# Loading per-edge data for four groups at once, and unrolling the loops of five engines to eight groups, in the second layer of a graph network

## The reference, cut to what matters

```
x[src]                                  # 32 features of the source, gathered
h = relu(w * w1 + b1)                   # 64 hidden values of the edge
R = [h, 1] @ w2m                        # 384 values of the edge
msg = products of R with x[src] and with x[src] turned by the frame (3 x 3)
out[dst] += msg                         # segment sum, here a scan along the sorted edges
```

## Time and profile before

| | us |
|---|---|
| median of three runs | 22618.37 |
| lowest and highest | 22526.03, 22643.42 |
| profiled execution, its span | 22701.8 |

### The profile page before, as it was taken

One profiled execution on the slowest core, in us unless ns is written; L12 is line 12 of the kernel. 1 busy time (PEld: TensorE's weight loads), 2 busy tenths in 40 slices (PEclk: granted clock), 3 DMA queues, 4 the chain that ended last, 5 costly groups with the idle time before them and its releaser, 6 DMA issues. The chain is left out here.

```text
span 22701.8 us, 347931 instructions
## 1 busy us (share of the span) xinstructions
PE 13867.1 (61%) x118841; PEld 8367.2 (37%) x118841; DVE 11327.4 (50%) x19891; ACT 2921.4 (13%) x4729; POOL 11857.2 (52%) x10101
## 2 busy tenths in 40 slices
PE   0465555555554767767676334444444449999999
PEld 0244433333333444444444222222222225555554
DVE  2665544444444777777777422222222234555554
ACT  0122222222220111111111001111111100000000
POOL 3588888888884555555555555555555620000000
PEclk6665555555556888888888667767776779999999
DMA  5444444444442222222222134444444424555555
GB/s 177 121 37 39 37 37 38 38 37 37 37 36 43 49 49 48 48 48 47 49 48 48 28 71 79 80 79 80 79 80 79 82 87 167 196 199 196 196 199 179
DMA packets 3839465, 1876.95 MB, mean 83 GB/s; under 512 B 2977892, under 2 KB 3534766, under 8 KB 3835982
## 3 DMA queue, kind: packets, MB, share of 16 engines
q1 hardware_dynamic: 1901390, 1398.07, 21.8%
q0 software_dynamic: 670464, 220.54, 11.2%
q10 hardware_dynamic: 1266578, 244.09, 6.4%
HBM read 1528.14 MB, written 397.72 MB: 85 GB/s over the span
## 5 line engine op out<-in xcount | busy, mean ns | idle before, releaser
L1958 POOL DMA_INDIRECT xg<-d_tab,s_i x3136 | 3283.1, 1047 | 2543.6 <-POOLq L1953 1373.0
L2843 PE MATMUL pacc<-nodes,HB 128*32 128x512 fp8e4 x70560 | 3938.2, 380 | 292.5 <-PEq L2887 281.6
L2501 POOL DMA_INDIRECT xag<-d_xa,s_i x3136 | 3009.5, 960 | 2031.2 <-POOLq L2497 1077.5
L2204 PE MATMUL pR<-w,H 128*128 128x384 f32 x6272 | 2666.3, 553 | 1585.7 <-PEq L2198 889.1
L1410 POOL DMA_INDIRECT d_acc<-AG,ix x1568 | 2475.4, 1579 | 518.7 <-issue 415.7
L1410 POOL DMA_INDIRECT d_acc<-T,ix x1568 | 2472.5, 1577 | 522.8 <-issue 435.0
L2843 PEld LDWEIGHTS pacc<-nodes,HB 128*32 128x32 bf16 x70560 | 1931.5, 97 | 2171.8 <-issue 317.4
L2630 PE MATMUL hb<-U,Wbc 128*128 128x512 f32 x784 | 614.7, 877 | 2816.2 <-PEq L2619 2672.1
L2528 DVE TENSOR_TENSOR_SCAN U<-mU,U,up 128x512 f32<-128x512 f32 x392 | 501.7, 1280 | 3632.8 <-DVEq L2527 3171.1
L2204 PEld LDWEIGHTS pR<-w,H 128*128 128x128 f32 x6272 | 1198.2, 211 | 2681.4 <-issue 2309.5
L1765 PE MATMUL pm<-ms,eq 128*128 128x32 f32 x6272 | 1366.0, 399 | 933.0 <-PEq L1763 928.7
(11 more groups left out here) (348 smaller groups left out, 17700.5 us busy)
## 6 DMA issues: line engine op xcount, KB each, us to landing
packed<-d_A SPq DMA_DIRECT2D x420, 1792.0 KB, 8.0
row<-d_m SPq DMA_DIRECT2D x1568, 64.0 KB
wrow<-d_w SPq DMA_DIRECT2D x196, 512.0 KB
d_scan<-so ACTq DMA_DIRECT2D x392, 256.0 KB
d_A<-stage ACTq DMA_DIRECT2D x96, 784.0 KB
d_exp<-zt SPq DMA_DIRECT2D x32, 1568.0 KB, 19.6
xe<-d_exp SPq DMA_DIRECT2D x196, 256.0 KB
xg<-d_tab,s_i POOLq DMA_INDIRECT x3136
```

The lines of the kernel that those rows point to most:

```text
L1958: e.indirect_dma_start(out=xg[k][:, t, :], out_offset=None, in_=d_tab, in_offset=bass.IndirectOffsetOnAxis(ap=s_i[n][:, t:t + 1], axis=0)) ...
L2204: last = e.matmul(pR[u % 2][:, j, 0:384], H[k][:, (2 * u + j) * P:(2 * u + j + 1) * P], w2[:, :], start=True, stop=True)
L2501: e.indirect_dma_start(out=xag[k][:, j * ST + c, :], out_offset=None, in_=d_xa, in_offset=bass.IndirectOffsetOnAxis(ap=s_i[n][:, col:col + ...
L2843: end = e.matmul(pacc[k][32 * g:32 * (g + 1), :], HB[i][:, b0 + bb, 32 * h:32 * (h + 1)], of, start=(begins and h == 0), stop=(ends and h ...
```

## The change

Ids, frames and flags get two buffers, each for four groups, in place of four for one group each: s_i is [128, 64], e9 has a dimension of four more, row is [128, 2048]. One transfer brings the ids of four groups (runs of 16 ids in place of 4), one the frames, and four the flags (runs of 2048 numbers). SP's order is rewritten. DVE and POOL wait for them at the first of four groups only, and ACT and PE free them at the last. The weights are loaded as before. As two buffers of four groups make a cycle of eight groups, the loop bodies of all five engines cover eight groups: 24 rounds in place of 48. The helpers scan_buffers, scan_dve and scan_back get a parameter wide, which is 1 in the other layers.

```diff
-            b = scan_buffers(st, DEEP, own=False)
+            b = scan_buffers(st, 2, own=False, wide=4)
-            s_i = [sb(st, f"s_i{n}", [P, T], I32) for n in range(DEEP)]
-            e9 = [sb(st, f"e9{n}", [P, 3, T, 3]) for n in range(DEEP)]
+            s_i = [sb(st, f"s_i{d}", [P, 4 * T], I32) for d in range(2)]
+            e9 = [sb(st, f"e9{d}", [P, 4, 3, T, 3]) for d in range(2)]
...
+                    def load(a_, d):
+                        e.wait_ge(S(f"fl{d}"), 1)
+                        e.sem_inc(S(f"fl{d}"), -1)
+                        e.dma_start(s_i[d][:, :].rearrange("p (c t) -> p c t", c=ST),
+                                    src_v[bass.ds(a_, 1), :, :, :].rearrange("a p c t -> (a p) c t")).then_inc(S(f"li{d}"), 16)
+                        e.wait_ge(S(f"fe{d}"), 1)
+                        e.sem_inc(S(f"fe{d}"), -1)
+                        e.dma_start(e9[d][:, :, :, :, :].rearrange("p s k t i -> p s (k t i)"),
+                                    d_fr[bass.ds(a_ * 4 + 4, 4), :, :].rearrange("s p x -> p s x")).then_inc(S(f"le{d}"), 16)
+
+                    def load_rows(a_, d):
+                        e.wait_ge(S(f"frow{d}"), 1)
+                        e.sem_inc(S(f"frow{d}"), -1)
+                        for c in range(ST):
+                            e.dma_start(b["row"][d][F * c:F * (c + 1), :], rows(m_v[c, bass.ds(a_ * 4 * SW, 4 * SW)], F)
+                                        ).then_inc(S(f"row{d}"), 16)
...
-                    with e.Fori(0, G // 4 - 1) as it:
-                        for n in range(4):
-                            load(it + (n + 3) // 4, (n + 3) % 4)
-                            load_row(e, b, it * 4 + n, n, m_v)
+                    with e.Fori(0, G // 8) as it:
+                        for d in range(2):
+                            load_w(it * 2 + d, 3)
+                            load(it * 2 + 1 + d, 1 - d)
+                            for n in range(3):
+                                load_w(it * 2 + 1 + d, n)
+                            load_rows(it * 2 + 1 + d, 1 - d)
...
-                    with e.Fori(0, G // 4 - 1) as it:
-                        for n in range(4):
-                            step((n + 1) % 4, it * 512 + ((n + 2) // 2 + 1) * 256)
+                    with e.Fori(0, G // 8) as it:
+                        for n in range(8):
+                            step((n + 1) % 8, it * 1024 + ((n + 2) // 2 + 1) * 256)
```

More of the change, by code:

```diff
@@ L1152, in load_row, with scan_buffers @@
                             ).then_inc(S(f"row{n}"), 16)
-        def scan_buffers(st, deep, own=True):
+        def scan_buffers(st, deep, own=True, wide=1):
             b = {}
-            b["row"] = [sb(st, f"row{n}", [P, SW]) for n in range(deep)]
+            b["row"] = [sb(st, f"row{n}", [P, wide * SW]) for n in range(deep)]
             b["sc"] = [sb(st, f"sc{k}", [P, SW]) for k in range(2)]
@@ new lines, in _ @@
+                    with e.Fori(0, G // 8) as it:
+                        for d in range(2):
+                            load_w(it * 2 + d, 3)
[3 more added lines that the diff above has]
+                            load_rows(it * 2 + 1 + d, 1 - d)
+                    load_w(G // 4 - 1, 3)
+                    for d in range(2):
+                        e.wait_ge(S(f"fl{d}"), 1)
+                        e.sem_inc(S(f"fl{d}"), -1)
+                        e.wait_ge(S(f"fe{d}"), 1)
+                        e.sem_inc(S(f"fe{d}"), -1)
@@ L2062, in tail, with scan, step @@
                                             ).then_inc(S(f"mg{k}"), 1)
[L2064 to L2069, removed]
+                    def scan(r):
+                        scan_dve(e, b, r, tp[r % 2][:, :], ALU.mult, ALU.add, wide=4)
+                        e.sem_inc(S(f"fmg{r % 2}"), 1)
+                    def step(r, count=0, first=False, last=False):
+                        k = r % 2
                         e.wait_ge(S("hf"), 1)
@@ L2084, in step @@
                                 if u in (1, 2, 3):
-                                    tail((n + 3) % 4, u - 1)
+                                    tail((r + 7) % 8, u - 1)
                                 if u == 6:
-                                    scan((n + 3) % 4)
+                                    scan((r + 7) % 8)
                             if u == 2 and not last:
-                                head((n + 1) % 4, count)
+                                head((r + 1) % 8, count)
                             if u > 2:
@@ L2159, in _ @@
                     spread(1)
-                    with e.Fori(0, G // 4 - 1) as it:
-                        for n in range(4):
+                    with e.Fori(0, G // 8) as it:
+                        for n in range(8):
                             hidden((n + 2) % 4)
                             early_sums((n + 1) % 2)
-                            spread((n + 2) % 4)
-                            scan_store(e, b, it * 4 + n, n % 2)
+                            spread((n + 2) % 8)
+                            scan_store(e, b, it * 8 + n, n % 2)
                     for n in range(2):
@@ L2247, in back, with step @@
                         last.then_inc(S(f"pb{k}"), 1)
-                    def step(n, past=2, last=False):
+                    def step(r, past=2, last=False):
+                        n = r % 4
                         radial(n, 0, past)
@@ L2252, in step @@
                         if past > 1:
-                            back((n + 2) % 4)
+                            back((r + 6) % 8)
                         radial(n, 2, past)
@@ L2259, in step @@
                         if past:
[L2260 removed]
+                            columns((r + 7) % 8)
                         radial(n, 5, past)
@@ L2271, in _ @@
                     step(1, past=1)
-                    with e.Fori(0, G // 4 - 1) as it:
-                        for n in range(4):
-                            step((n + 2) % 4)
+                    with e.Fori(0, G // 8) as it:
+                        for n in range(8):
+                            step((n + 2) % 8)
                     step(2)
```

101 lines of the change are left out of this document (50 added, 51 removed).

## The result

The changed kernel takes 22706.32 us (median of 12 runs, 22651.73 to 22749.67), the kernel before 22619.67 us (12 runs, 22526.03 to 22670.55). The ratio is 1.0038, 95% interval 1.0026 to 1.005: 87 us slower, under the bound of 0.5%. The time lies 56 us above the forecast of 22650 and inside both ranges.

A forecast was written before the change was run, and what follows sets the result against it. The prediction took the second layer to be bound by DVE's work plus 1365 us of waits. All terms were 0 except 32 us of fetch pauses: 22734 us, scaled by 0.9963 to 22650 us (+0.14%), range 22430 to 22800.

The forecast's parts named there:

- What bounds the kernel: Second layer: DVE's own work sets the quick step, 21.70 us; 1365 us are DVE waiting, mostly for PE's products.
- A body twice as long: DVE's second-layer loop: some 540 instructions are fetched anew each round, 24 pauses, 0 to 65 us, taken as 32 us lost.
- Fewer waits, half the back-edges: Second-layer loops: fewer queue waits and increments gain 0 to 5 us, taken as 0; 24 branches instead of 48, 0.
- Fewer transfers and the new order on SP: SP in the second layer: 878 issues saved, covered by its 2740 us wait, and no load late; both 0.
- Rival A: Second-layer stalls of 1365 us shrink with SP's transfers, by 256 us, to 22394 us; chance 0.25.
- Rival B: DVE's loop: fetching costs more than one short pause a round, time 22745 or 22877 us; chance 0.15.
- Rival C: DVE's loop: body fits or is fetched ahead, 22618 us less up to 5; counted within the forecast's 0.50.
- Rival D: Second-layer steps lock differently, either sign, up to 507 us more; chance 0.10, split 0.02 faster and 0.08 slower.
- The signs: Profile after: q14 transfers, DVE idle past its branch, longer SP waits, step near 28.9 us; wrong if moved over 0.6 us.

The follow-up runs named there:

- run 12: The changed kernel with a back-edge hint at the head of DVE's second-layer loop, on a chip that stalls, against the kernel before: 22857.35 against 22717.3 us, 1.0053.
- run 6: The kernel before with every second of a group's 16 gathers left out in the second layer, output differs, against the kernel before: 20127.14 us, 0.9953.
- run 1: The kernel before with DVE's loop alone covering eight groups, against the kernel before, chip without stalls: 20256.72 against 20249.01 us, 1.0001.
- run 7: The kernel before with DVE's loop alone covering eight groups, repeated on another chip without stalls, against the kernel before: 20222.97 against 20232.37 us, 0.9997.
- run 5: The changed kernel again, unaltered, against the kernel before on a chip without stalls: 20220.76 against 20234.76 us, 0.9995.
- run 10: The changed kernel with a back-edge hint at the head of DVE's second-layer loop, against the kernel before, chip without stalls: 20196.21 against 20215.13 us, 0.9987.
- Run 4: The changed kernel with three waits and one increment a group taken out of DVE's queue, against the kernel before, chip without stalls: 20243.06 us, 0.9997.
- run 2: The kernel before with the loops of SP, POOL, ACT and PE covering eight groups, DVE's still four, against the kernel before: 20244.64 us, 0.9997.
- run 3: The kernel before with ids, frames and flags loaded for two groups at once, loops of four groups, against the kernel before: 20316.23 us, 1.0036.
- run 8: The kernel before with second-layer flags loaded only for the first four groups, output differs, against the kernel before: 20322.44 against 20232.37 us, 1.0041.

## Why the prediction came out as it did

The forecast was 32 us of loss, the measured one is 87 (59 to 113 by the interval). The size is inside the range, and the sign and the class are right, but the sum is a third of what was lost, and most of the loss has another cause than the one that was summed. With the summed cause taken away, run 12 still loses 140 us. So that the forecast and the loss have the same sign is largely luck.

- **What bounds the kernel.** Right: the quick step is DVE's 21.6 us before and after, and run 6 shows it. Not seen was that the rest, 1365 us, is there on some chips and not on others with the same code. One trace of before could not show that. It could show POOL's waits for `half`, 196 us in the layer, which the prediction left out where it took POOL's waits for xg and for ids.
- **A body twice as long.** Right in every part that rows show: 539 instructions for the forecast 540, about six transfers on q14 a round for some five, a pause just past the branch in DVE and none that shows in PE (1398 instructions a round; beside those of q14 only two instruction transfers run in 5300 us), and runs 1 and 7 tie it to the length of DVE's body alone. The size was well placed. Without stalls a branch step of the changed kernel takes 23.53 us, the others about 21.8: 1.7 x 24 = 41 us gross, in a range of 0 to 65. But net of the waits for sources that it replaces, it is nothing that can be told in runs 1, 5 and 7, and some 16 us by the hint of run 10 (0.9987 against run 5's 0.9995, on two chips, their intervals overlapping: 0.0008 x 20215). The likeness to 562 was enough; where the limit lies was not settled. The Trainium skill, page "Runtime: NRT & Kernel Launch", section "Instruction fetch mechanics", puts DVE's window at 512 instructions, and makes it of two blocks of 256. By that rule a body of 507 would stay only if it began within the first few instructions of a block; no trace shows where it begins. Run 4 has a body of 507 fetched each round, and 277 is not, so in this kernel the length that a loop can keep lies between them.
- **Fewer waits, half the back-edges.** Costed at 0. No run separates them; without stalls, run 2 leaves room for 0.12% faster to 0.06% slower for the longer loops of four engines.
- **Fewer transfers and the new order on SP, costed at 0.** Here the sum fell short: one of the parts at nothing, these or the eight-group loops of the other engines, is not nothing where the steps stall. The argument was that no load is late, and it held: POOL's waits for ids are 0.6 us, DVE has none for frames or flags. What it left out is that the 1365 us of stalls need not stay as they are when no load is late. With the change the place in the step at which stalls stand moves: from u = 0 and 1, where 36 steps become 4, and in part from u = 4 and 5, to u = 2, where 2 become 57. There PE's increment of `half` has been given, POOL keeps gathering, and these steps take 39.0 us, where those at u = 0 and 1 took 34.6. Run 12 shows that the loss stays with the pause removed. That it comes through `half` is read from three traces (waits at u = 2 of 25, 713 and 842 us; POOL's for `half` of 189.9, 24.0 and 27.3 us), and no run moved `half` alone.
- **Rival A**, stalls that shrink with the transfers: not borne out. With fewer transfers DVE's waits went from 1276 to 1338 us, and on the other chips runs 3 and 8 became slower with fewer, by 0.36% and 0.41%.
- **Rival B**, dearer fetching: fell. Without stalls the gross 41 us is below its 113; where the steps stall, the long steps with a branch (34.0 us) are made up by the short ones behind them (23.2), and with the pause removed run 12 loses no less.
- **Rival C**, no fetch: fell with q14.
- **Rival D**, steps that lock differently, is what the larger part of the loss looks like. It had 0.10 and a mechanism in half a sentence, a pause in DVE each eighth step. The pause is not the driver, as run 12 shows. What is left of the change are the positions of the loads, the fewer waits and the eight-group loops; none of them was separated on a chip that stalls, because runs 1 to 3 fell on one that doesn't.
- **The signs.** The mean step was to be near 28.9 and came out at 29.13, under the 0.6 us named as the point of failure. SP's waits grew as forecast, from 2599 us to 4091 in 7300 to 12600 us. No sign was named for a stall that changes its place.

Open: what holds back PE's results and DVE's operands while POOL gathers, why only some chips show it, and which part of the change moves the stall. A test would put `half` at another position, and the old order of loads beside the eight-group loops, on a chip that stalls.

## What to carry to other kernels

Before an edit is costed at nothing because no load is late, look at what shares its beat with the stall that dominates. Here one engine's permission to go on (`half`) decides how long another engine's run of gathers is, and steps with the stall on one side of it take 34.6 us, on the other 39.0. Count the instructions of an unrolled loop body; on DVE a body of 507 was fetched anew each round and one of 277 was not, and a hint of the back-edge took the pause away (0.9987 to the kernel before). And measure a small change on more than one chip: 1.0038 on one and 0.9995 on another are the same edit.

## What the hardware showed beside that

- The same kernel has medians of 20215 to 20249 us on four chips, and of 22620 and 22717 in the two other sets of runs. The difference sits nearly all in the second and third layers, the two with gathers through POOL: 28.7 against 22.1 us a step in the second, 4985.7 against 3922 us for the third layer's scans. What comes before the second layer's first scan takes 7105 to 7168 us in all traces, though POOL issues indirect transfers there too, which scatter; what comes behind the third layer's last scan takes 4458 to 4472.
- With four of seven transfers a group gone, POOL's own time for a gather fell from 1070 to 984 ns, and the kernel became slower.
- From a taken branch to the next instruction of its queue DVE needs a median of 4.3 us (2.9 to 4.8) in the changed kernel, whose body is fetched anew, 3.5 us in runs 1 and 7, 0.29 us in the kernel before and 0.60 us with the hint.
